# Aggregation begun without the fifth row tile, head 0 of two tiles ahead, and layer 0's weighted products row tile by row tile

## The reference

```
x = x + segment_sum((layernorm(x) @ W)[row] * norm, col) + b        # layer 0, graph convolution

xn  = rmsnorm(layernorm(x), norm1_w)                                 # layer 0, attention: q = k = v = xn
qkv = xn.reshape(b, s, 12, 64).transpose(0, 2, 1, 3)
scores = einsum('bhqd,bhkd->bhqk', qkv, qkv) / sqrt(64)
ao  = einsum('bhqk,bhkd->bhqd', softmax(scores), qkv)
out = layernorm(x) + ao
...                                                                  # top-2 of 8 experts and a shared expert
```

## Time and profile before

| | us |
|---|---|
| median of three runs (lowest, highest) | 1574.85 (1572.22, 1582.6) |
| the profiled execution, its own time | 1572.62 |
| its span in the profile | 1571.1 |
| PE busy | 1455.7 (93%) |
| DVE busy | 1257.5 (80%) |
| ACT busy | 884.6 (56%) |
| POOL busy | 323.2 (21%) |

### The profile page before, as it was taken

The page is one execution under the profiler, slowest core; times in us unless marked ns, Lnnn a source line. Parts: engine busy times, 40 slices in busy tenths (PEclk is TensorE's granted clock), DMA queues, the critical chain, the costliest instruction groups (busy, mean ns, idle before and its releaser), DMA issues.

```text
span 1571.1 us, 36911 instructions
## 1 busy us (share of the span) xinstructions
PE 1455.7 (93%) x14608; PEld 1260.3 (80%) x14608; DVE 1257.5 (80%) x2191; ACT 884.6 (56%) x1285; POOL 323.2 (21%) x251
## 2 busy tenths in 40 slices
PE   7999788887999999999999799859999999999996
PEld 6777566665668899999997644448899999999994
DVE  8999767765566788888888889877978888888885
ACT  5114377775345676677773345545566666666651
POOL 1000146650300000000004067734600000000050
PEclk9999989998999999999999889959999999999999
DMA  7650000005656788888884011029888888888793
GB/s 201 151 131 13 11 1 2 1 1 182 180 194 205 283 287 295 305 296 292 310 289 129 17 34 32 19 97 336 275 292 301 292 298 281 306 288 296 280 282 92
DMA packets 55556, 297.61 MB, mean 189 GB/s; under 512 B 14063, under 2 KB 14319, under 8 KB 32433
## 3 DMA queue, kind: packets, MB, share of 16 engines
q1 hardware_dynamic: 41761, 263.23, 49.1%
q0 software_dynamic: 13712, 33.26, 7.7%
HBM read 264.07 MB, written 32.34 MB: 189 GB/s over the span
## 4 chain that ended last, share of the span: by engine, by line
PE 71%; DVE 18%; POOL 3%; ACT 3%; issue 3%; DMA 1%; DVEq 0%; POOLq 0%; ACTq 0%; SPq 0%
PE ps L771 14%; PE ps L750 10%; PE ps L752 10%; PE ps L754 9%; PE ps L2403 5%; PE ps L2386 5%; DVE wl L1466 3%; DVE wl L1467 3%; POOL wl L1021 2%; PE ps L2515 2%; PE ps L2315 2%; PE ps L2201 2%; PE ps L783 2%; DVE wl L627 1%; PE ps L2301 1%
## 5 line engine op out<-in xcount | busy, mean ns | idle before, releaser
L750 PE MATMUL ps<-big,wh 128*128 128x176 f16 x2160 | 496.3, 240 | 8.2 <-DVE wl L627 6.2
L754 PE MATMUL ps<-big,wl 128*128 128x176 f16 x2160 | 496.4, 238 | 0.0
L752 PE MATMUL ps<-big,wh 128*128 128x176 f16 x2160 | 496.4, 238 | 0.0
L771 PE MATMUL ps<-big,wh 128*128 128x176 f16 x2160 | 262.7, 238 | 1.2 <-DVE big L661 1.2
L771 PE MATMUL ps<-big,wl 128*128 128x176 f16 x1080 | 248.9, 239 | 0.0
L627 DVE SCALAR_TENSOR_TENSOR wl<-ext,wh 128x2304 f16<-128x2304 f32 x90 | 229.7, 2552 | 1.3 <-issue 1.1
L627 DVE SCALAR_TENSOR_TENSOR wl<-raw,wh 128x2304 f16<-128x2304 f32 x90 | 229.5, 2550 | 0.0
L546 ACT ACTIVATE wh<-raw 128x2304 f16<-128x2304 f32 x90 | 190.4, 2117 | 59.2 <-PE ps L771 54.2
L750 PEld LDWEIGHTS ps<-big,wh 128*128 128x128 f16 x2160 | 208.7, 97 | 11.9 <-DVE wl L627 6.0
L546 ACT ACTIVATE wh<-ext 128x2304 f16<-128x2304 f32 x90 | 190.5, 2117 | 48.9 <-PE ps L771 35.0
L752 PEld LDWEIGHTS ps<-big,wh 128*128 128x128 f16 x2160 | 211.2, 98 | 0.2
(11 more groups left out here) (379 smaller groups left out, 2781.0 us busy)
## 6 DMA issues: line engine op xcount, KB each, us to landing
raw<-in_units SPq DMA_DIRECT2D x54, 1152.0 KB, 5.4
ext<-in_units SPq DMA_DIRECT2D x54, 1152.0 KB, 5.5
raw<-in_units SPq DMA_DIRECT2D x36, 1153.0 KB, 5.7
ext<-in_units SPq DMA_DIRECT2D x36, 1153.0 KB, 6.0
raw<-in_units_s SPq DMA_DIRECT2D x16, 769.0 KB, 4.5
ext<-in_units_s SPq DMA_DIRECT2D x16, 769.0 KB, 4.5
x_slots<-logs SPq DMA_DIRECT2D x1, 8976.0 KB
big<-x_slots POOLq DMA_DIRECT2D x17, 528.0 KB, 8.5
```

Source lines behind the costliest of these rows:

```text
L750: nc.tensor.matmul(o, wh[:, u % RING, w_], x_, start=c == 0 and m == 0, stop=False, skip_group_check=True)
L752: nc.tensor.matmul(o, wh[:, u % RING, w_], xTl[:, c, 0:ph.n], start=False, stop=False, skip_group_check=True)
L754: ins = nc.tensor.matmul(o, wl[:, u % RING, w_], x_, start=False, stop=c == KC - 1, skip_group_check=True)
L771: ins = nc.tensor.matmul(o, l_[:, u % RING, w_], r_, start=first and k == 0 and c % 2 == 0, stop=last and k == 2, skip_group_check=True)
```

## The change

- TensorE's aggregation is reordered: for tile 0, all products with input tiles 0 to 3 come first, after a wait for `htl` of tile 3, then those with input tile 4 after its own wait. The other tiles have the order of parts changed, not the number of matmuls.
- Of tiles 3 and 4 only head 0 is split ahead of the attention. VectorE weights only 64 columns of tile 4 there. The rest is moved into the first steps: `heads_high(3)` behind the side copy, `heads_high(4)` behind the first exponential, `row_out(3)` and `row_out(4)` behind the second and third, the rest of `row_weighted_1(4)` behind VectorE's side copy, and both `heads_low` behind the second maximum.
- `pT` becomes ten blocks of 5x125 columns, one for each row tile of two heads. `tile_weighted` forms the product of one row tile with all keys, three steps after its scores' step: ten matmuls of 125 columns, each step one tile. The sums of the five row tiles lie 128 columns apart in banks 6 and 7. The first tile of a head waits for `sum_out` of the head before (`s_mout`), the last for `fin` (`s_mfin`).
- `sum_out(h-1)` moves on ScalarE from the first step of head h+1 to the fourth of head h, behind the exponential; `sum_back` is cut in three tiles and two, in the fifth step of head h and the first of head h+1.

```diff
--- before.py
+++ after.py
@@ -200,7 +200,7 @@
         outn = big[0:P, 6340:6340 + NT * HD].rearrange("p (t e) -> p t e", t=NT)
-        pT = ext[0:P, 0:6250].bitcast(F16).rearrange("p (s q k n) -> p s q k n", s=2, q=2, k=NT)
+        pT = ext[0:P, 0:6250].bitcast(F16).rearrange("p (s q k n) -> p s q k n", s=2, q=2 * NT, k=NT)
         ident16 = sb("ident16", [128, 128], F16)
@@ -272,6 +272,10 @@
             return bank(4)[0:P, 0:3 * P], bank(5)[0:P, 0:2 * P]
+        def weighted_tiles():
+            return bank(6, 2)[:, 0:NT * 128].rearrange("p (t n) -> p t n", t=NT)[:, :, 0:P]
@@ -981,10 +985,8 @@
-                h, t = divmod(n, NT)
                 pool.wait_ge(s_whi, n + 1)
-                own = slice(t * P, (t + 1) * P)
-                nc.gpsimd.tensor_tensor(pT[:, 1, h % 2, :, own], key_blocks(n), pT[:, 0, h % 2, :, own],
+                nc.gpsimd.tensor_tensor(pT[:, 1, n % (2 * NT), :, :], key_blocks(n), pT[:, 0, n % (2 * NT), :, :],
                                         ALU.subtract).then_inc(s_wlo, 1)
@@ -1136,10 +1138,11 @@
                 act.wait_ge(s_var, count["sq"])
-                if t + 1 < NT:
+                if t + 2 < NT:
                     heads_high(t, 0, H)
                     row_out(t)
-            heads_high(NT - 1, 0, 1)
+                else:
+                    heads_high(t, 0, 1)
@@ -1160,36 +1163,37 @@
-                h, t = divmod(n, NT)
                 act.wait_ge(s_wTv, 2 * n + 2)
-                if t == 0 and h >= 2:
-                    act.wait_ge(s_mpv, (h - 1) * NT)
-                nc.scalar.activation(pT[:, 0, h % 2, :, t * P:(t + 1) * P], key_blocks(n), ACT.Copy).then_inc(s_whi, 1)
+                if n >= 2 * NT:
+                    act.wait_ge(s_mpv, n - 2 * NT + 1)
+                nc.scalar.activation(pT[:, 0, n % (2 * NT), :, :], key_blocks(n), ACT.Copy).then_inc(s_whi, 1)
...
                     act.wait_ge(s_mback, h)
-                nc.scalar.activation(outT, bank(6, 2)[:, 0:T], ACT.Copy).then_inc(s_mout, 1)
+                nc.scalar.activation(outT.rearrange("p (t n) -> p t n", t=NT), weighted_tiles(), ACT.Copy).then_inc(s_mout, 1)
             side_out(0)
-            heads_high(NT - 1, 1, H)
-            row_out(NT - 1)
+            heads_high(NT - 2, 1, H)
             for n in range(H * NT):
...
                 weights(n)
+                if n == 0:
+                    heads_high(NT - 1, 1, H)
+                if n in (1, 2):
+                    row_out(NT - 3 + n)
+                if t == 3 and h:
+                    sum_out(h - 1)
                 if n:
...
                     side_out(h + 1)
-                if t == 0 and h >= 2:
-                    sum_out(h - 2)
                 if h in (6, 10):
...
                     squares((h - 6) // 4, t)
-            sum_out(H - 2)
             weight_high(H * NT - 1)
@@ -1599,10 +1603,10 @@
-            def row_weighted_1(t):
-
-                return nc.vector.scalar_tensor_tensor(out=xw[:, t, :], in0=xres[:, t, :], scalar=mv[:, t, 0:1],
-                                                      in1=vec[:, 1, :], op0=ALU.subtract, op1=ALU.mult)
+            def row_weighted_1(t, n0=0, n1=D):
+                return nc.vector.scalar_tensor_tensor(out=xw[:, t, n0:n1], in0=xres[:, t, n0:n1], scalar=mv[:, t, 0:1],
+                                                      in1=vec[:, 1, n0:n1], op0=ALU.subtract, op1=ALU.mult)
@@ -1650,12 +1654,15 @@
                                                op0=ALU.mult, op1=ALU.mult).then_inc(s_var, 1)
-                if more_:
+                if t + 2 < NT:
                     row_weighted_1(t + 1)
...
                     heads_low(t, 0, H)
-            dve.wait_ge(s_vh, 2 * NT - 1)
-            heads_low(NT - 1, 0, 1)
+                elif more_:
+                    row_weighted_1(t + 1, 0, HD)
+            for t in (NT - 2, NT - 1):
+                dve.wait_ge(s_vh, 2 * t + 1)
+                heads_low(t, 0, 1)
@@ -1695,12 +1702,15 @@
             side_out(0)
-            dve.wait_ge(s_vh, 2 * NT + 1)
-            heads_low(NT - 1, 1, H)
+            row_weighted_1(NT - 1, HD, D)
             masked_counts(NT - 1)
...
                 top(n)
+                if n == 1:
+                    for k in (NT - 2, NT - 1):
+                        dve.wait_ge(s_vh, 2 * k + 5)
+                        heads_low(k, 1, H)
                 if n:
@@ -2236,18 +2246,29 @@
             counts_turned(3)
+            def aggregate(i, n0, n1, k0, k1):
+                o = aggregated(i, n0, n1)
+                for l_, r_ in ((CTh, hth), (CTh, htl), (CTl, hth)):
+                    for k in range(k0, k1):
+                        ins = nc.tensor.matmul(o, l_[:, k, i * P:(i + 1) * P], r_[:, k, n0:n1],
+                                               start=l_ is CTh and r_ is hth and k == 0,
+                                               stop=l_ is CTl and k == NT - 1)
+                return ins
+            pe.wait_ge(s_nl, NL_H[NT - 2] + 1)
+            pe.wait_ge(s_aggv, 3)
+            for n0, n1 in ((0, BANK), (BANK, D)):
+                aggregate(0, n0, n1, 0, NT - 1)
             pe.wait_ge(s_nl, NL_H[NT - 1] + 1)
-            for i in range(NT):
-                pe.wait_ge(s_aggv, NT + i - 1 if i else 3)
+            for n0, n1 in ((0, BANK), (BANK, D)):
+                ins = aggregate(0, n0, n1, NT - 1, NT)
+            ins.then_inc(s_agg, 1)
+            for i in range(1, NT):
+                pe.wait_ge(s_aggv, NT + i - 1)
                 for n0, n1 in ((0, BANK), (BANK, D)):
-                    o = aggregated(i, n0, n1)
-                    for r_ in (hth, htl):
-                        for k in range(NT):
-                            nc.tensor.matmul(o, CTh[:, k, i * P:(i + 1) * P], r_[:, k, n0:n1],
-                                             start=r_ is hth and k == 0, stop=False)
-                    for k in range(NT):
-                        ins = nc.tensor.matmul(o, CTl[:, k, i * P:(i + 1) * P], hth[:, k, n0:n1], start=False,
-                                               stop=k == NT - 1)
+                    ins = aggregate(i, n0, n1, 0, NT)
                     if n1 == D or i == NT - 1:
@@ -2262,8 +2283,8 @@
                         if h == 1:
-                            pe.wait_ge(s_vl, NT + 1)
-                            pe.wait_ge(s_vh, 2 * NT + 2)
+                            pe.wait_ge(s_vl, NT + 2)
+                            pe.wait_ge(s_vh, 2 * NT + 4)
                         ins = nc.tensor.transpose(side_bank(s)[:, t, :],
@@ -2302,31 +2323,33 @@
-            def weighted_chunk(h, t):
-
-                if t == 0:
-                    if h:
-                        pe.wait_ge(s_mout, h)
-                        pe.wait_ge(s_mfin, h)
-                    pe.wait_ge(s_wlo, h * NT + NT)
-                v = vst[t][:, h, 0:2, :].rearrange("p c e -> p (c e)")
-                for s in range(2):
-                    for n0, n1 in ((0, BANK), (BANK, T)):
-                        ins = nc.tensor.matmul(bank(6, 2)[:, n0:n1], v, pT[:, s, h % 2, t, n0:n1],
-                                               start=t == 0 and s == 0, stop=t == NT - 1 and s == 1)
+            def tile_weighted(n):
+                h, t = divmod(n, NT)
+                if t == 0 and h:
+                    pe.wait_ge(s_mout, h)
+                if t == NT - 1 and h:
+                    pe.wait_ge(s_mfin, h)
+                pe.wait_ge(s_wlo, n + 1)
+                for k in range(NT):
+                    v = vst[k][:, h, 0:2, :].rearrange("p c e -> p (c e)")
+                    for s in range(2):
+                        ins = nc.tensor.matmul(weighted_tiles()[:, t, :], v, pT[:, s, n % (2 * NT), k, :],
+                                               start=k == 0 and s == 0, stop=k == NT - 1 and s == 1)
                 ins.then_inc(s_mpv, 1)
-            def sum_back(h):
+            def sum_back(h, t0, t1):
                 pe.wait_ge(s_mout, h + 1)
-                for t in range(NT):
+                for t in range(t0, t1):
                     ins = nc.tensor.matmul(bank(7)[0:P, 128 + t * HD:128 + (t + 1) * HD], outT[:, t * P:(t + 1) * P],
                                            both[:, :], start=True, stop=True)
-                ins.then_inc(s_mback, 1)
+                if t1 == NT:
+                    ins.then_inc(s_mback, 1)
...
             scores(0)
-            for n in range((H + 1) * NT + 2):
+            for n in range(H * NT + 3):
                 h, t = divmod(n, NT)
@@ -2334,11 +2357,13 @@
                     sides_transposed(h + 1)
-                if t == 1 and h >= 2:
-                    sum_back(h - 2)
-                if 1 <= h <= H:
-                    for k in ((), (), (0,), (1, 2), (3, 4))[t]:
-                        weighted_chunk(h - 1, k)
+                if n >= 3:
+                    tile_weighted(n - 3)
+                if t == NT - 1 and h:
+                    sum_back(h - 1, 0, 3)
+                if t == 0 and h >= 2:
```

(2 more changed lines are left out.)

## The result

| | before | after |
|---|---|---|
| median of 20 runs each (lowest, highest), us | 1576.54 (1570.75, 1582.6) | 1571.37 (1565.06, 1578.0) |
| profiled execution, its own time (span) | 1572.62 (1571.1) | 1573.86 (1572.3) |
| PE, DVE, ACT busy | 1455.7, 1257.5, 884.6 | 1459.1, 1254.0, 885.8 |

The ratio of the times is 0.9968, with a 95% interval of [0.9953, 0.9983]: some 5 us of 1577, real but well within 1%. The prediction said 1570 within 1563 to 1578. The profiled execution of after is 1.2 us *longer* than that of before, though, so the span can't be used to explain the median. The stage that the diff touches has to be read by itself.

The account below looks back on a forecast made before the run. No engine was taken as full: waits between engines bound aggregation, handover and heads. Terms -1.9 - 2.8 - 0.8 + 1.5 = -4.0 us gave 1568.6 from the profiled execution, 1570.8 from the median; forecast 1570, range 1563 to 1578.

Parts of the forecast that it names:

- A: Aggregation: tile 0 starts without waiting for row tile 4, moving VectorE's chain behind it; -1.9 us.
- B: Handover to attention: only head 0 of tiles 3 and 4 goes ahead, so the first exponential comes sooner; -2.8 us.
- The thin cover: Head 0: TensorE's scores and transposes, 2.28 us, hide work pushed between exponentials, 2.30; uncovered, 3.6 us lost.
- C: Attention heads: weighted products by row tile, 0.56 us a tile, bring a head to 12.06 us; sum -0.8 us.
- W: TensorE's weighted products in a head: the first waits for `sum_out` until 3.19 us after the side transposes.
- two delays of 0.2 by `squares`: Heads 6 and 10: ScalarE's `squares` push exponential 3 by some 0.2 us each; +0.4 us.
- The tail: Attention's end: `sum_out(11)` stays behind `squares` and a table load, last `sum_back` at the lower clock; +1.5 us.
- (1): Attention: weight loads set the pace of the new weighted products; 1584 us or, at the upper bound, 1603; chances 0.07, 0.03.
- (3): Attention: TensorE's clock falls inside heads, 3 us more a head, 33 in eleven; 1603 us; chance 0.04.
- (4): Head 0 fills up with pushed work, so A and B don't reach the attention's end; 4.7 lost, 1575 us; chance 0.12.
- (5): Between aggregation and head 0: the clock stays up over the gap, saving some 2 us; 1568 us; chance 0.08.
- (2): Attention heads: the wait for `s_mout` doesn't bind, a head takes 11.2 us; 1561 us; chance 0.06.

Follow-up runs that it names:

- part_a: Kernel before with only the aggregation of tile 0 begun early; 1575.57 us, ratio 0.9995 to before.
- part_b: Kernel before with only the heads of tiles 3 and 4 split, head 0 ahead of the attention; 1577.18 us, ratio 1.0000 to before.
- tail_first: Changed kernel with the last `sum_out` ahead of ScalarE's wait for `head_joined(10)`, the last `squares` and table load; 1569.31 us, ratio 0.9946 to before.
- rows_later: Changed kernel with the two `row_out` in steps 6 and 9, not 1 and 2; exponential 0 to head 1's side transposes 5.71 us, against 5.64.
- sum_first: Changed kernel with `sum_out(h-1)` ahead of the exponential in a head's fourth step, not behind it; 1563.78 us, ratio 0.9912 to before.
- both_first: Changed kernel with the `sum_out` orders of sum_first and tail_first together; 1563.5 us, ratio 0.9909 to before.
- parts_ab: Kernel before with the early aggregation and the split heads, without weighted products by row tile; 1571.48 us, ratio 0.9976 to before.
- part_c: Kernel before with only weighted products by row tile and `sum_out` and `sum_back` moved; 1574.88 us, ratio 0.9991 to before.
- w_ahead: both_first with the weighted products ahead of the side transposes in a head's third step; 1560.13 us in one run, beside 1568.42 of before.

## Why the prediction was right

The number came out right, 1570 against 1571.37, and so did the sum in which it was made: -4.0 was predicted and -4.73 is measured at the attention's end. That the total lies within 1.4 us is in part luck. It was built on three runs of before with a median of 1574.85, and 20 runs give 1576.54, from which the same sum makes 1572.5; the measured interval allows anything from -2.7 to -7.4 us. The terms, one by one:

- **A: -1.9 predicted, -1.97 measured**, in after and alone in part_a. The first L2255 was to stand at 160.8; it stands at 161.42, but the origin is 0.63 later in that execution, which makes it 160.79.
- **B: -2.8 predicted, -2.73 measured** up to exponential 0 (-2.64 alone in part_b). VectorE's share was to be 1.83 and is 1.83 (25.16 to 23.33 in the rows above); the rest, some 1.0 on ScalarE, is 0.90. The exponential was to come near 195.6; 196.27 less the 0.63 is 195.64. The thin cover held: S(3) was to start 2.28 after S(2) and starts 2.31 after it (197.19 to 199.50), without a wait. No table load came with `row_out`. The Trainium skill (ScalarE: Activation LUTs, Table sets: the hidden batching unit), by which identity is in every set, agrees with the trace: the only load at this stage is that of 194.97.
- **C in the heads: -0.8 predicted, -1.0 measured.** The schedule drawn by hand gave 12.06 for a head, and 12.05 is measured; `sum_out` at 2.47 behind the side transposes (2.49) and W at 3.19 (3.23). The 57 ns of the side transposes and the 55.5 worked out from the expert layers were the right rows: a tile takes 0.56. The Trainium skill (TensorE: Matmul & The Clock Gate, Back-to-back issue gap) gives some 81 ns for such a stream; ten in 0.56 us are 56, and the measurement decides. Of the two delays of 0.2 by `squares`, that of head 6 came (12.23 against 12.05), that of head 10 lies in the tail, where its exponential 3 comes 1.90 behind the side transposes instead of 1.72. Head 0 did take W into its holes: from the side transposes of head 1 to those of head 2 it is 10.51 in before and 10.52 in after.
- **The tail: +1.5 predicted, +1.20 measured**, by its own parts: `sum_out(11)` stands 24.96 behind the last side transposes, 24.79 in before, so 0.17 instead of 0.4; and `sum_back` to the end takes 2.39 (346.77 to 349.16) instead of 1.34, so +1.05 where +1.1 was expected. That ScalarE's chain was the cause of the idle time is shown by tail_first: with the order changed the 3.97 are 0.78 and the loss is gone. That `sum_back` is slow because of the clock is read from the traces, 0.50 over its 2.36 in after and 1.00 over its 1.30 in before. How much of the +1.05 is the change's own doing is less certain: with the old tail's code the same ten matmuls took 1.30 to 2.26 us in four executions, and the term is this large because that of before had the full clock there. That it came out as forecast is luck to this extent.

**The rivals.** (1), the pace of weight loads, falls with 0.56 a tile. (3) falls: the clock stayed at 1.00 over the head of 12.05, with its 0.76 of wait. (4) falls with rows_later and part_b: 0.07 and 0.09 us more or less in head 0, which is inside the scatter of 0.3, and not the 4.7 that were to be lost. (5) falls: the clock went down over the gap here as well, to 0.68 in 186 to 202, and S comes every 1.08 us there (193.57 to 194.65) instead of every 0.54. (2) was wrong for this kernel and right as a lever. It gave a head of 11.2 and 1561 us; sum_first, where the wait is indeed gone, has 11.38, and its ratio of 0.9912 on 1574.85 is 1561.0. The sentence that the order of VectorE and ScalarE "gives no way to it" holds for the order as written. I had worked out the place of `sum_out`, 2.47, and not asked whether it had to be there: ahead of exponential 3 it costs that one 0.36 and gives TensorE 0.92.

What the prediction missed is only visible from the other end: it said nothing of how far one profiled execution may be trusted. The one of after took 1573.86, 5.3 above the 1568.6 that the sum made of the one of before. Had only the two profiles been at hand, a right sum would have looked wrong.

## What to carry to other kernels

Draw one period by hand with the distances of the old trace, and for each wait that it shows ask what stands ahead of its releaser on that engine, and which of the two another engine waits for more: here the place of one instruction of 0.7 us was worth 6.3 us, more than the restructuring around it (4.7), measured with the restructuring done. Work that is finished sooner is worth nothing where its consumer is queued behind other things, as at the end of the attention. Judge a change of 5 us in 1570 by distances from a common point ahead of it to a common point behind it, and only then by medians; and find out first by how much such a distance differs between executions of the same code, here 0.3 us in head 0 and 0.8 in the tail.

## What the runs showed that I had not expected

**The same code differs by 5 us between executions.** Windows of layer 1's graph attention (from the first to the last of its products, L2515 before, L2540 after; columns as in the earlier trace rows), which no kernel here changes. After, before and both_first:

```profile
900.70:1029.80 129.10, 116.41 (x445) 59.62 (x446) 105.68 (x228) 65.59 (x135) 88.64 (x70) 0.87 0.09 26
```

```profile
902.50:1027.20 124.70, 112.81 (x446) 57.20 (x446) 108.66 (x228) 66.05 (x135) 88.71 (x70) 0.90 0.09 27
```

```profile
891.70:1016.30 124.60, 112.73 (x445) 57.12 (x446) 108.62 (x228) 66.01 (x135) 88.64 (x70) 0.90 0.09 27
```

| | part_a | both_first | before | tail_first | parts_ab | part_c | sum_first | w_ahead | part_b | after | rows_later |
|---|---|---|---|---|---|---|---|---|---|---|---|
| us | 123.8 | 124.6 | 124.7 | 126.2 | 126.7 | 127.8 | 127.9 | 127.9 | 127.9 | 129.1 | 129.1 |
| granted clock | 0.89 | 0.90 | 0.90 | 0.90 | 0.88 | 0.88 | 0.87 | 0.88 | 0.87 | 0.87 | 0.87 |

The stage takes 123.8 to 129.1 us, and nearly always longer where the granted clock is lower: 4.4 of the 5.3 us that after took longer behind its attention lie here. What decides which clock an execution gets in this stage stays open; each column is one execution. It is no trait of the changed kernel, whose median is lower, and fits the 12 to 13 us over which 20 runs of either kernel scatter.

**The last `sum_back` got one level of the clock, the other, or a mixture.** It is always ten matmuls of 128x64. The idle time is that right ahead of it, the clock is the granted one over its own length:

| | before | part_b | tail_first | parts_ab | w_ahead | part_a | both_first | after | part_c | rows_later | sum_first |
|---|---|---|---|---|---|---|---|---|---|---|---|
| idle ahead, us | 0.78 | 1.84 | 0.78 | 1.85 | 0.78 | 1.84 | 0.78 | 3.97 | 3.97 | 3.98 | 3.98 |
| `sum_back`, us | 1.30 | 1.44 | 1.55 | 2.06 | 2.16 | 2.26 | 2.36 | 2.36 | 2.36 | 2.36 | 2.36 |
| granted clock | 1.00 | 0.86 | 0.80 | 0.58 | 0.56 | 0.53 | 0.50 | 0.50 | 0.50 | 0.50 | 0.50 |

The length follows the clock from column to column. Behind the gaps of 3.97 and 3.98 us the clock was 0.50 four times of four. Behind the shorter ones it was anything: 1.84 us went with 0.86 in part_b and with 0.53 in part_a, 0.78 with 1.00 in before and with 0.50 in both_first. So a gap just ahead doesn't tell what a short group behind it will take; what decides it in the shorter cases stays open.
